# Filling products on TensorE between the stages of a four-layer transformer kernel on one core

## The reference

```python
x = x + jnp.tanh(g_xattn[1]) * _L1_xattn_ref(_layernorm(x, axis=-1), ctx_1024, ctx_1024, ...)
x = x + jnp.tanh(g_ffn[1]) * _L1_ffn_ref(_layernorm(x, axis=-1), L1_ffn_Wg, ...)
```

## Time and profile before

| | |
|---|---|
| median of three runs | 2131.59 us |
| the profiled execution | 2132.82 us |
| its span, from the first instruction to the last | 2130.8 us |
| TensorE busy | 1866.5 us, 88% |
| VectorE busy | 1452.2 us, 68% |
| ScalarE busy | 1055.7 us, 50% |
| GpSimd busy | 718.9 us, 34% |
| mean granted TensorE clock | 0.920 |

### The profile page before, as it was taken

The page is one execution under the profiler, slowest core; times in us unless marked ns, Lnnn a source line. Parts: engine busy times, 40 slices in busy tenths (PEclk is TensorE's granted clock), DMA queues, the critical chain, the costliest instruction groups (busy, mean ns, idle before and its releaser), DMA issues.

```text
span 2130.8 us, 31747 instructions
## 1 busy us (share of the span) xinstructions
PE 1866.5 (88%) x9982; PEld 1591.9 (75%) x9982; DVE 1452.2 (68%) x2416; ACT 1055.7 (50%) x1863; POOL 718.9 (34%) x732
## 2 busy tenths in 40 slices
PE   5659996796999999999999999999776994894994
PEld 3459996685788888888888888888556994783994
DVE  4847776677777777777777777777654665665674
ACT  4327774344555555554545455555234762342771
POOL 3012331436344434444443444342002322421331
PEclk8859998897999999999999999999876997895997
DMA  3035662100000000000000000030113433002553
GB/s 117 9 105 187 194 186 84 36 1 28 18 31 15 30 30 30 15 30 30 30 15 30 30 26 19 30 133 20 42 58 111 151 107 100 1 1 89 150 161 131
DMA packets 113564, 138.74 MB, mean 65 GB/s; under 512 B 15332, under 2 KB 101606, under 8 KB 113504
## 3 DMA queue, kind: packets, MB, share of 16 engines
q1 hardware_dynamic: 105952, 121.70, 18.0%
q0 software_dynamic: 7552, 16.24, 2.7%
HBM read 117.22 MB, written 24.90 MB: 67 GB/s over the span
## 4 chain that ended last, share of the span: by engine, by line
PE 70%; DVE 10%; issue 10%; ACT 4%; POOL 3%; DMA 2%; SPq 0%; ACTq 0%; DVEq 0%; POOLq 0%
PE ps L647 37%; PE ps L843 10%; PE ps L844 10%; PE ps L845 10%; POOL sc L530 2%; PE ps L658 1%; POOL xs L526 1%; ACT ps L1379 1%; DVE xs L1923 1%; DVE bn L1475 1%; ACT wsplit L1364 1%; PE ps L1002 1%; PE ps L1043 1%; DVE lnx L1468 1%; DVE wsplit L1894 1%
## 5 line engine op out<-in xcount | busy, mean ns | idle before, releaser
L647 PE MATMUL ps<-h_hi,wsplit 128*128 128x512 f32 (+3 forms) x2016 | 588.9, 350 | 1.8 <-DVE xT L1682 1.3
L647 PEld LDWEIGHTS ps<-h_hi,wsplit 128*128 128x128 f32 x2016 | 366.8, 188 | 48.3 <-DVE xT L1682 1.7
L647 PE MATMUL ps<-h_lo,wsplit 128*128 128x512 f32 (+3 forms) x1008 | 352.1, 349 | 0.0
L535 POOL TENSOR_TENSOR wsplit<-wraw,zero 128x256 fp32r<-128x256 f32 (+2 forms) x160 | 151.9, 966 | 501.2 <-PE ps L845 411.7
L1290 ACT ACTIVATE lnx<-ps 128x512 f32<-128x512 f32 x384 | 229.0, 597 | 106.3 <-PE ps L845 64.1
L647 PE MATMUL ps<-xTh,wsplit 128*128 128x256 f32 (+2 forms) x992 | 259.3, 315 | 13.4 <-DVE h_lo L1875 7.0
L1682 DVE TENSOR_TENSOR xT<-xT,ps 128x1024 f32<-128x1024 f32 x124 | 151.5, 1222 | 122.2 <-PE ps L647 122.2
L1299 ACT ACTIVATE h_act<-h_act 128x512 f32<-128x512 f32 x192 | 120.9, 630 | 213.9 <-DVE h_act L1660 213.7
L1303 ACT ACTIVATE h_hi<-ps 128x512 fp32r<-128x512 f32 x256 | 152.7, 596 | 143.0 <-PE ps L647 141.8
L1875 DVE TENSOR_TENSOR h_lo<-ps,h_hi 128x256 fp32r<-128x256 f32 (+2 forms) x248 | 117.4, 473 | 154.3 <-ACT h_hi L1383 149.0
L843 PE MATMUL ps<-xTh,wsplit 128*128 128x512 f32 x512 | 204.3, 399 | 5.4 <-ACT lnx L1290 3.5
(11 more groups left out here) (283 smaller groups left out, 3611.5 us busy)
## 6 DMA issues: line engine op xcount, KB each, us to landing
wraw<-in_L_w SPq DMA_DIRECT2D x124, 512.0 KB, 3.6
wraw<-in_L_ffn_Wg SPq DMA_DIRECT2D x32, 256.0 KB, 2.7
wraw<-in_L_ffn_Wu SPq DMA_DIRECT2D x32, 256.0 KB, 3.2
wraw<-in_L_ffn_Wd SPq DMA_DIRECT2D x32, 256.0 KB, 3.6
x_tok<-lnx SPq DMA_DIRECT2D x12, 512.0 KB, 3.8
lnx<-y_tok SPq DMA_DIRECT2D x12, 512.0 KB, 6.4
y_tok<-lnx SPq DMA_DIRECT2D x3, 2048.0 KB, 13.7
wat<-in_attn SPq DMA_DIRECT2D x16, 256.0 KB, 5.1
```

Of the source, the lines that this page charges most:

```text
L535: return pool.tensor_tensor(out_, in_, zero[:, :].to_broadcast(shape), ALU.add)
L647: return pe.matmul(out_, lhsT, rhs, start=start, stop=stop)
```

## The change

TensorE gets products whose result nobody reads: `fill(bank, count)` issues `count` products of 128 x 128 by 128 x 256 in bf16, both operands being the identity matrix read as bf16, into a bank of `ps` that is free there. Each such product has a weight load of its own. Three waits are added, behind which a filling begins: in attn1 and attn3 on `x_done` less 6 tiles, in attn2 on `x_done` less 2 tiles, and in the first group of ffn1 on `xt_done`. No other engine's program is changed, and nothing of TensorE's own work is moved or removed.

```diff
@@ -646,6 +646,13 @@
+    filler = ident[:, :].bitcast(BF16)
+    def fill(bank, count):
+        for _ in range(count):
+            pe.matmul(ps[:, bank, 0:2 * P], filler[:, 0:P], filler, start=True, stop=True)
     def turn_norm(n, wide=False, after=None):
@@ -668,6 +675,7 @@
     last.then_inc(ctx_tr, 1)
+    fill(6, 28)
@@ -721,6 +729,7 @@
         turn(3)
+        fill(7, 16)
         pe.wait_ge(a0_k, 2)
@@ -739,12 +748,16 @@
                 query(s + 2)
+            fill(7, 22)
             project(s)
+        fill(7, 70)
     attn0()
...
         pe.wait_ge(m_tab, 5 * m + 2)
+        pe.wait_ge(x_done, NT * n - 6)
+        fill(0, 24)
         pe.wait_ge(x_done, NT * n)
@@ -810,7 +823,11 @@
                 query(i + 2)
+            else:
+                fill(0, 6)
             turn_probs(i, j)
+            if not ahead:
+                fill(0, 6)
             if not first:
@@ -822,13 +839,16 @@
         scores(1)
+        fill(7, 32)
         step(0, 0, first=True)
...
         step(NT - 1, 1, ahead=False)
+        fill(0, 6)
         turn_heads(NT - 1)
         output(NT - 1)
+        fill(0, 26)
@@ -870,6 +890,8 @@
             product(1, 2, z, tp, True)
+            if first:
+                fill(UC, 24)
             need_x("11")
@@ -895,6 +917,9 @@
                 last.then_inc(p_down, 1)
+            if first:
+                pe.wait_ge(xt_done, NG * (n + 1))
+                fill(7, 40)
             pe.wait_ge(p_copy, 6 * G + COPY["u5"])
@@ -969,9 +994,12 @@
                     last = mm(ps[:, 4, i * E:(i + 1) * E], xT[:, k, i * P:(i + 1) * P], wr[:, layer, k, :], k == 0, k == KD - 1)
+                if i < NT - 1:
+                    fill(7, 1)
             if g == NG - 1:
...
         turn_norm(n, after=router)
+        fill(7, 28 if TOPK[layer] == 1 else 42)
@@ -983,6 +1011,7 @@
         last.then_inc(r_rank, 1)
+        fill(7, {0: 52, 2: 32, 3: 48}[layer])
@@ -993,6 +1022,7 @@
         last.then_inc(r_tok, 1)
+        fill(4, 44)
@@ -1059,6 +1089,7 @@
         turn_rows(0, 0)
+        fill(4, 10)
         expert(0, 0, start=True)
@@ -1079,6 +1110,8 @@
     def attn2(n):
+        pe.wait_ge(x_done, NT * n - 2)
+        fill(7, 32)
         turn_norm(n)
@@ -1106,6 +1139,7 @@
         last.then_inc(a2_pe, 1)
+        fill(7, 34)
         pe.wait_ge(a2_act, 2 + NG)
@@ -1117,6 +1151,7 @@
         last.then_inc(a2_pe, 1)
+        fill(7, 18)
         pe.wait_ge(a2_dve, 13)
```

## The result

The changed kernel takes 2121.77 us (median of 20 runs, 2109.56 to 2124.12), against 2131.28 us (20 runs, 2120.1 to 2139.82) for the kernel before: 0.9949 of it, 95% interval 0.9932 to 0.9966. It is faster, but by 10 us and not by the 42 forecast, and 2121.8 lies outside the range of 2074 to 2116. The 20 runs fall into two groups: 16 at 2120.6 to 2124.1 us with a mean granted clock of 0.949 to 0.952, and 4 at 2109.6 to 2112.1 us with 0.957 to 0.958. The profiled execution took 2121.08 us with a span of 2119.0.

A forecast was written before the change was run, and what follows sets the result against it. TensorE was taken as the bound, with waits dropping its clock to 0.50 in stretches where the next engine waits for it; stage savings summed to 42.3 us, from 2132.8 to 2090, range 2074 to 2116.

The forecast's parts named there:

- The routers: Routers of ffn0, ffn2 and ffn3: at the upper clock they save 4, 5.2 and 2 us.
- I take half, -4: ffn0's router: -8.5 us, or less if the clock falls in the empty 4.0 us ahead; half taken, -4.
- the filling holds the clock, but not across what is left: Rival, every stage: empty stretches remain, half the stretches stay low, only 15 to 25 us kept, 2108 to 2118; chance 0.2.
- the routers stay low: Rival, three routers: transposes, 8-column products and single fillings don't hold the clock; 11.2 us lost, 2106; chance 0.12.
- transposes hold the clock: Transposes count as work holding the clock, since it rose in ffn2 behind 16 f32 transposes in 3.35 us.
- The 24 ahead of K and V: Start of attn1 and attn3: all 24 run on TensorE's path, 2.6 us upper or 5.1 lower clock; counted as nothing.
- with it I count nothing: attn1 and attn3: GpSimd's 13.13 us of bias work covers K and V coming 1 to 3 us later; cost 0.
- up to 5 us each: attn1 and attn3: the loss in each stage if GpSimd's bias work did not cover the late K and V.
- its busy time times (1 less its clock): Rule for every stretch: its saving from the upper clock is TensorE's busy time times 1 less its clock.
- Slower: Rival, all stages: mostly-zero products don't raise the clock, each costs 0.213 us; +66 us, 2199; chance 0.04.
- no effect: Rival, all stages: other engines pace them, so the time stays at 2127 to 2137 us; chance 0.05.
- ideal: Whole kernel at the upper clock, the start's savings left out: -51 us, 2082; basis for the lower end, 2074.

The follow-up runs named there:

- e4_two_per_tile: The changed kernel with a filling product behind each of a tile's two router products (31 a router instead of 15); 2103.37 us, 0.9843.
- e10_closed_no_singles: `e5_closed` without the 15 single filling products in each router; 2100.39 us, 0.9862.
- e9_only_attn0: The changed kernel with one number changed: 104 filling products for 70 behind attn0; 2110.41 us, 0.9913.
- the second profile: The changed kernel, unchanged, profiled once more beside the kernel before; 2113.69 us (one run).
- e7_all_early24: `e5_closed` with two router products a tile, the 24 ahead of the waits on in_wat and m_tab, 16 behind the norm's transposes; 2094.30 us, 0.9826.
- e5_closed: The changed kernel with more filling at four stage ends: 104 for 70, 36 and 46 for 26, 56 for 40; 2097.10 us, 0.9844.

## Why the prediction was wrong

**The routers (forecast -11.2, measured +10.0 with the choice of experts behind them) are 21 of the 30 us missed.** The step that failed is "I take half, -4" for ffn0 and its absence for the other two. I saw the empty 4.0 us and the projection at 0.68 behind a wait of that size, and still costed ffn2 and ffn3 as if filling ahead meant a router at the upper level. Across all profiles the count is plain. With filling in the router and at most 1.05 us empty ahead of it, 28 of 28 routers were at the upper level, from 11.4 to 11.8 us. With single products and 1.9 to 3.9 us empty, 9 of 14 took some 20 us, and the 5 others 11.4 to 12.5. In the traces of these 14 the clock fell 0.9 to 1.4 us ahead of the router's first transpose or 1.1 to 1.6 us behind it in the nine slow ones, which stayed low to their end; in three of the fast ones it fell between 0.5 us ahead and 0.3 us behind and was up again 3.0 to 3.7 us in; in two it did not fall, or only in the last 0.3 us. What sets the moment of the fall was not found. My rival "the filling holds the clock, but not across what is left" named this, at 2108 to 2118 and with a chance of 0.2; its time was too low, because it took each miss as the loss of a gain, whereas two routers that had been partly at the upper level before (16.8 and 13.7 us) fell to 20. The rival "the routers stay low" was right in outcome and half right in cause. The wait ahead brings the clock down: with single products and closed ends it stayed up. That it stays down is a matter of density: one product a tile did not raise it in the nine, though it rose in three others, where the fall came close to the router's start; two a tile raised it in all three of `e4_two_per_tile`.

That transposes hold the clock, as I counted, came out both ways. In `e10_closed_no_singles` the routers of ffn0 and ffn3, without single products, fell from 1.00 to 0.50 some 5.7 and 5.9 us in, with 0.17 and 1.04 us empty ahead; ffn2's, with 0.13 us empty ahead, was at 1.00 for all 10.89 us on transposes and 8-column products. What told them apart was not found. In `e9_only_attn0` closing the wait from 3.89 to 0.18 us, with the router's own instructions unchanged, was enough for 1.00 over ffn0's whole router.

**The 24 ahead of K and V (forecast 0, measured +5.6 and +4.3) are the second miss, 10 us.** The reading was right: they stand behind `ctxD`, all 24 on TensorE's path, at the lower clock, 5.28 us. The step that failed is the cover: GpSimd's bias work, and "with it I count nothing". The cover hides the first scores alone. The next query behind the second scores started 16.3 us behind the release before (391.53 less 375.21):

```profile
391.53 1.16 PE L647 MATMUL ps<-xT,wat 128*128 128x128 f32 x8
```

Now the 32, which stand in its place, start 22.9 us behind it (388.81 less 365.90), 6.6 later: 5.1 for the 24, and 1.5 while the clock was low from 381.6 on. They put what follows off by 5.0 us, not 3.4. I had used the same 5.60 us of waiting twice, for the lateness of K and V and for the 32. Together they need 6.6 and 5.0, which is 6.0 more than there is; `turn_probs` came 5.7 us late, since the query between took 0.3 less. The bound that I named myself, "up to 5 us each", was the answer.

**ffn1 (forecast -3, measured +0.4).** The rule "its busy time times (1 less its clock)" was used on a stretch in which VectorE works for 15.16 of 17.0 us. The clock rose to 0.81 and the stretch did not get shorter; the row said so.

**The experts.** They start at the upper clock (1.00, against 0.50), and in 3.80 us TensorE is busy for 3.03: most of the rest it waits for VectorE's lower halves, as the forecast expected. Measured -1.1 and -0.6 in ffn2 and ffn3 and +1.5 and +1.3 in the second profile, against -1.5 each; in ffn0 the pace of the occasion covers it.

**What held.** No run shows the 0.107 us of a filling product at the upper clock: it was my estimate, about half of the 0.21 of the earlier trace rows, and the kernel before's own products of 256 columns start 0.12 us apart at that clock (161.08, 161.20, 161.31, at 1.00). But the price held: filling products start 0.109 to 0.110 us apart at the upper clock (the 70 behind attn0) and 0.213 to 0.214 at the lower (the 24 of attn1), against 0.107 and 0.213 forecast. So did, against the profile that the terms came from, the first steps of attn1 and attn3 (each 11.8 to 5.9), attn2, and the ends of attn1 and attn3. "Slower" and "no effect" did not come. The sum came out too, but not by its terms, which is in part luck: with the ends closed, the 24 out of the path, two products a tile in the routers and 16 more in attn1 and attn3 the span falls by 39.2 us (`e7_all_early24`). There the routers bring more (17.9, not 11.2), and attn0, ffn1 and the experts less. The "ideal" of -51 at the range's lower end does not follow from the terms shown: these give 42.3, the other 4.5 of ffn0's router and 0.5 of the experts, 47.3. The forecast was for a kernel whose fillings reach across the waits, and this one's did not.

**One more weakness** is that the earlier trace rows is one execution. In two more profiles of the kernel before, attn1's first two steps took 12.5 us (16.3 in the first), attn3's 10.8 and 15.6 (16.4), and ffn3's router 19.9 and 13.8 (13.7). Terms taken from one trace were up to 6 us off either way, though the three spans agree to 3.3 us. Against those two profiles "attn1, the rest" gains 1.9 and 1.8 us in the changed kernel and not 6.6, "attn3, the rest" loses 0.9 or gains 6.4, and ffn3's +5.8 is -0.3 against the one with the slow router.

## What to carry to other kernels

Here a filling that ended 1.9 to 3.9 us before the work that it should speed up left that work slow in 9 of 14 cases; make it reach close to the end of the wait, and read in the trace whether it does. Before adding work "into a wait", look at what the wait's releaser itself waits for, and give each microsecond of cover to one thing only. Judge a stretch's clock from several profiles, since one execution of the same kernel can have a router at 11 us and the next at 20.

## What the runs showed of the hardware that was not expected

- A filling product between the router's f32 products is almost free. Fifteen cost 0.47 us at the upper clock (ffn2's router, 11.36 with and 10.89 without) and 0.6 at the lower, 0.03 to 0.04 each, against 0.109 and 0.213 by itself. The router's products have 8 columns and a weight load of 128 columns in f32 each, and PEld is busy for 10.87 of the 11.36 us of ffn0's router in `e5_closed`. That the filling's columns lie beside those loads is my guess from these numbers; no run shows it. The 1.6 us counted for each router were three times too much.
- The granted clock of the same stretch differs between executions of the same program. Where 32 filling products were followed by a wait of 0.3 to 3.1 us ahead of `turn_probs`, the next two steps were at the upper clock in 8 of 14 stages and took 5 to 6 us more in the 6 others; where they ran up against it with no wait, they were at the upper clock in 18 of 18. So it is with a whole router: ffn3's in the changed kernel took 19.75 us at 0.54 in one profile and 11.36 us at 1.00 in the other.
- ffn0's expert loop has two steady paces, 5 to 6 us apart over the stage. Among the kernels with filling they went with the occasion, or the chip, and not with the kernel. What sets them was not found.
